# Turning the second weight by transposing transfers of pairs of 8-bit values

## The reference

```python
x = L0_attn_x                                   # (2, 16384, 1024) float32
x = x + layernorm(attention(layernorm(x), Wq, Wk, Wv, Wo))
x = x + layernorm(ffn(layernorm(x), fast_b, w_fc, w_proj, u, v, gate))

def bitlinear(x, w):                            # w: rows are output features
    scale = clip(mean(abs(w), axis=1), 1e-5)
    tern = clip(round(w / scale), -1, 1)        # -1, 0 or 1
    return x @ (tern * scale).T
def ffn(x):
    h = bitlinear(x, w_fc) + gate * (x @ v.T @ fast_b.T @ u.T)   # hidden 4096
    return bitlinear(maximum(h, 0) ** 2, w_proj)                 # back to 1024
```

## Time and profile before

| what | value |
|---|---|
| median of 3 runs | 1131.83 us (1131.32 to 1132.46) |
| the profiled execution, its own time | 1133.4 us |
| its span on the slowest core (core 0) | 1131.9 us |
| spans of the 8 cores | 1122.7 to 1131.9 us |
| mean granted TensorE clock, by core | 0.969 to 0.973 of full |
| PE busy, core 0 | 1054.5 us (93%) |
| DVE busy, ACT busy | 577.5 us (51%), 411.8 us (36%) |

### The profile page before, as it was taken

How to read it: one execution, slowest core, us unless ns; L and a number is a source line. 1 busy time by engine, 2 the same in 40 slices (tenths; PEclk the granted TensorE clock), 3 DMA queues, 4 the chain that set the end, 5 groups by cost and what they waited for, 6 DMA issues and landing times.

```text
span 1131.9 us, 16149 instructions; the slowest of 8 cores (1122.7 to 1131.9 us)
## 1 busy us (share of the span) xinstructions
PE 1054.5 (93%) x5477; PEld 494.7 (44%) x5477; DVE 577.5 (51%) x904; ACT 411.8 (36%) x761; POOL 15.9 (1%) x33
## 2 busy tenths in 40 slices
PE   3788848978999999999999999999999999999997
PEld 1222335534444444544445444454445444444443
DVE  3888789676334443454435353444435554444333
ACT  4677699324322243213422144212422243114300
POOL 0000000000000000000000000000000000000000
PEclk9988968989999999999999999999999999999999
DMA  8999997483113212231022310341005210221011
GB/s 256 209 235 226 215 232 204 117 204 113 20 38 96 91 38 38 75 106 62 1 57 67 120 38 1 93 131 60 16 19 124 101 38 1 79 70 38 1 59 54
DMA packets 61172, 105.99 MB, mean 94 GB/s; under 512 B 37261, under 2 KB 37517, under 8 KB 61092
## 3 DMA queue, kind: packets, MB, share of 16 engines
q1 hardware_dynamic: 57124, 92.63, 29.2%
q0 software_dynamic: 3728, 12.25, 6.1%
q10 hardware_dynamic: 240, 0.07, 0.0%
HBM read 87.79 MB, written 17.31 MB: 93 GB/s over the span
## 4 chain that ended last, share of the span: by engine, by line
PE 85%; DVE 5%; issue 4%; DMA 3%; ACT 1%; SPq 1%; DVEq 0%; ACTq 0%; POOLq 0%
PE fcb L449 37%; PE pjp L463 35%; PE xp L463 1%; PE xp L503 1%; PE xp L601 1%; PE xp L562 1%; PE fcb L463 1%; PE pt L433 1%; DMA r<-x 1%; DVE below L1188 1%; DMA stg<-wpj 1%; PE pjp L514 1%; DMA lrow<-ctx 1%; DMA xy<-wpj 1%; PE xp L651 0%
## 5 line engine op out<-in xcount | busy, mean ns | idle before, releaser
L449 PE MATMUL fcb<-xnT,Sfc 128*128 128x512 bf16 x2048 | 466.1, 386 | 6.0 <-DVE r L1136 3.9
L463 PE MATMUL pjp<-Spj,r 128*128 128x512 fp8e4 x1920 | 426.6, 381 | 0.0
L449 PEld LDWEIGHTS fcb<-xnT,Sfc 128*128 128x128 bf16 x2048 | 197.4, 99 | 254.5 <-issue 33.4
L463 PEld LDWEIGHTS pjp<-Spj,r 128*128 128x128 bf16 x1920 | 185.8, 98 | 222.3 <-issue 8.0
L1136 DVE TENSOR_TENSOR r<-fcb,rpp 128x512 bf16<-128x512 f32 x224 | 154.5, 691 | 242.9 <-ACT rpp L827 242.5
L827 ACT ACTIVATE rpp<-fcb,hsc 128x512 f32<-128x512 f32 x224 | 153.5, 687 | 222.3 <-PE fcb L449 220.2
L1108 DVE TENSOR_TENSOR xy<-pjp,oscb 128x512 f32<-128x512 f32 x60 | 41.3, 689 | 162.0 <-PE pjp L463 161.9
L816 ACT ACTIVATE xnT<-pt 128x1024 bf16<-128x1024 bf16 x32 | 32.7, 1020 | 138.4 <-PE pt L433 138.3
L799 ACT ACTIVATE lv<-mv,cvecs 128x1 f32<-128x1 f32 x64 | 18.8, 293 | 153.2 <-DVE mv L1081 86.0
L1113 DVE BATCH_NORM_STATS2 s<-xy 128x6 f32<-128x512 f32 x64 | 44.4, 694 | 9.4 <-DVE xy L1108 6.0
L1130 DVE TENSOR_TENSOR xy<-xy 128x1024 f32<-128x1024 f32 x32 | 39.1, 1223 | 4.3 <-DVE xy L1122 4.3
(11 more groups left out here) (143 smaller groups left out, 608.4 us busy)
## 6 DMA issues: line engine op xcount, KB each, us to landing
out<-xy SPq DMA_DIRECT2D x32, 512.0 KB, 3.0
xy<-x SPq DMA_DIRECT2D x31, 512.0 KB, 4.3
xs<-x SPq DMA_DIRECT2D x29, 512.0 KB, 4.5
xy<-wfc SPq DMA_DIRECT2D x16, 512.0 KB, 5.5
xy<-wpj SPq DMA_DIRECT2D x13, 512.0 KB, 5.7
stg<-wpj SPq DMA_DIRECT2D x11, 512.0 KB, 5.1
stg<-wfc SPq DMA_DIRECT2D x10, 512.0 KB, 5.2
xs<-wpj SPq DMA_DIRECT2D x8, 512.0 KB, 6.4
```

The costliest lines, as they stand in the source:

```text
L449: mm = te.matmul(fcb[n % 3][:, 0:TT], s_fc[:, dci * HF + hc * 128:dci * HF + hc * 128 + 128], xnT[:, dci * TT:(dci + 1) * TT], start=(dci ...
L463: mm = te.matmul(dst, r2[:, hc * TT + s * 128:hc * TT + s * 128 + 128], s_pj[:, hc * D + half * 512: hc * D + half * 512 + 512], start=(hc ...
```

## The change

The turn of the second weight leaves PE and ACT and becomes 32 more transposing transfers from SP. DVE writes `tern` of units 32 to 63 as 8-bit values, 1,024 bytes per partition; the transfer takes them for 512 columns of 16-bit values and transposes those. So two neighbouring columns of w_proj land interleaved, byte by byte, in one partition of `s_pj`; the host puts columns c and c+128 side by side beforehand, and `proj_part` reads its 512 moving columns at every second byte. `unit`, `evac` and their semaphores `p_un` and `a_ev` go. `cut(n)` now always waits for the transfer of unit n-3; PE waits for the transfers (`weights_in`) at n = 48 and ahead of `proj(0, 1)`; SP issues the last nine in a loop of its own, with the loads of `xs` between them; GpSimd's `rows(0)` waits for the last three transfers.

```diff
-        tbank = [b.bitcast(BF16) for b in pjb]
+        spj_pair = s_pj[:].bitcast(BF16).rearrange("p (c o) -> p c o", o=D)
+        spj_even = s_pj[:].rearrange("p (c o e) -> p c e o", o=D, e=2)
+        tern8 = [t[:, 0:D // 2].bitcast(FP8) for t in tern]
...
+            def turned(m):
+                if m < NFU:
+                    sync.dma_start_transpose(
+                        sfc3[:, :, m * 128:m * 128 + 128], tern[m % 3][:]
+                    ).then_inc(d_tr[m % 3], 16)
+                else:
+                    q, k = divmod(m - NFU, 4)
+                    sync.dma_start_transpose(
+                        spj_pair[:, 4 * k:4 * k + 4, q * 128:q * 128 + 128],
+                        tern[m % 3][:, 0:D // 2]
+                    ).then_inc(d_tr[m % 3], 16)
...
                 if m >= 0:
                     sync.wait_ge(v_ab, m + 1)
-                    if m < NFU:
-                        sync.dma_start_transpose(
-                            sfc3[:, :, m * 128:m * 128 + 128], tern[m % 3][:]
-                        ).then_inc(d_tr[m % 3], 16)
+                    turned(m)
...
-            sync.wait_ge(v_ab, NUNIT - 2)
-            load(xs[0], 4, d_xs[0])
-            sync.wait_ge(v_ab, NUNIT - 1)
-            load(xs[1], 5, d_xs[1])
-            sync.wait_ge(v_ab, NUNIT)
+            for m in range(NUNIT - NSLOT, NUNIT):
+                sync.wait_ge(v_ab, m + 1)
+                turned(m)
+                if m == NUNIT - 2:
+                    load(xs[0], 4, d_xs[0])
+                if m == NUNIT - 1:
+                    load(xs[1], 5, d_xs[1])
...
-            gp.wait_ge(p_un, NPU)
+            for n in range(NUNIT - 3, NUNIT):
+                gp.wait_ge(d_tr[n % 3], 16 * (n // 3 + 1))
...
-                        s_pj[:, hc * D + half * 512:
-                             hc * D + half * 512 + 512],
+                        spj_even[:, hc // 2, hc % 2,
+                                 half * 512:half * 512 + 512],
...
-            def unit(n):
-                if n > NFU + 1:
-                    te.wait_ge(a_ev, n - NFU - 1)
-                te.wait_ge(v_ab, n + 1)
-                for blk in range(DCN):
-                    cols = slice(blk * 128, blk * 128 + 128)
-                    mm = te.transpose(tbank[n % 2][:, cols],
-                                      tern[n % 3][:, cols], identb[:])
-                mm.then_inc(p_un, 1)
+            def weights_in(n):
+                for m in range(n - 3, n):
+                    te.wait_ge(d_tr[m % 3], 16 * (m // 3 + 1))
...
-                if n >= NFU:
-                    unit(n)
...
                     if m == 0:
-                        te.wait_ge(a_ev, 16)
+                        weights_in(NFU + 16)
...
-            te.wait_ge(a_ev, NPU)
+            weights_in(NUNIT)
...
-                if n >= NFU:
-                    evac(n)
...
-                if n >= NFU + 3:
-                    ve.wait_ge(p_un, n - NFU - 2)
-                elif n > 2:
+                if n > 2:
                     ve.wait_ge(d_tr[n % 3], 16 * (n // 3))
...
-                ve.scalar_tensor_tensor(tern[n % 3][:], stg[n % NSLOT][:],
+                dst, sat = ((tern[n % 3][:], None) if n < NFU else
+                            (tern8[n % 3], False))
+                ve.scalar_tensor_tensor(dst, stg[n % NSLOT][:],
...
-        "wpj": np.ascontiguousarray(np.asarray(w_proj, np.float32)),
+        "wpj": np.ascontiguousarray(np.asarray(w_proj, np.float32).reshape(
+            D, HCN // 2, 2, 128).transpose(0, 1, 3, 2).reshape(D, HF)),
```

More of the change, by code:

```diff
@@ L230, in build_nc @@
         v_lr = sem("v_lr")
-        p_un = sem("p_un")
         p_early = sem("p_early")
-        a_ev = sem("a_ev")
         p_osc = sem("p_osc")
@@ L844, in abssum @@
                               accum_out=wsum[:, n:n + 1]).then_inc(a_abs, 1)
[L846 to L852, removed]
             def out_scale(half):
@@ L1197, in cut @@
                                              ALU.is_lt))
-                ve.scalar_tensor_tensor(tern[n % 3][:], stg[n % NSLOT][:],
+                dst, sat = ((tern[n % 3][:], None) if n < NFU else
+                            (tern8[n % 3], False))
+                ve.scalar_tensor_tensor(dst, stg[n % NSLOT][:],
                                         thr[:, c:c + 1], below[n % 2][:],
-                                        ALU.is_gt,
-                                        ALU.subtract).then_inc(v_ab, 1)
+                                        ALU.is_gt, ALU.subtract,
+                                        saturate=sat).then_inc(v_ab, 1)
             def stats(g, src):
```

## The result

| what | before | after |
|---|---|---|
| median of 4 runs each | 1131.57 us | 1143.03 us (1142.17 to 1144.24) |
| ratio, 95% interval | 1 | 1.0104 (1.0092 to 1.0116) |
| profiled execution, its own time | 1133.4 us | 1143.09 us |

What follows compares the result with a forecast made beforehand. PE is held by the two large products for most of the span; DVE paces the first stage's units, PE barely behind. Start -0.5, restart +1.2, pace +4.1 give +4.8 us: median 1131.8 to 1136.6, range 1131 to 1145.

Steps and rivals of the forecast that it cites:

- What goes and what does not follow: End of first stage: 6.8 us of turning leave PE's chain, early parts end at 207.5, but proj(0, 1) awaits the last transfer.
- The pace: Cuts of the second weight: DMA share sets 2.46 us a unit against DVE's 2.28, delaying the last cut 4.1 us.
- The landing of the last transfer: Ahead of proj(0, 1): the last transfer takes 3.8 us, so the start is 0.5 us earlier, apart from the pace.
- The restart: At proj(0, 1): PE idles before it and restarts at the lower clock, costing 1.2 us.
- The zeros: Strided read, 8-bit write, later xs load, GpSimd's rows(0) and SP's issue times: each taken to cost zero.
- The strided read: Second product, line 463: reading every second byte costs zero; the rival, 4 us from 1% on, 415 if doubled, had 0.09.
- the 8-bit write: DVE's tern: 8-bit output taken to change nothing from 1284 ns; the rival of a faster write had 0.07.
- The queue saturates hard: Rival on the transfers: pace 2.73 us a unit, delay 10.4 us, +11.1 in all, 1142.9 us; chance 0.14.
- The DMA engines keep up: Rival on the transfers: pace at or below DVE's, delay 0 to 1.5 us, 1132.5 to 1134 us; chance 0.27.

Runs made afterwards that it cites:

- merged: The changed kernel with two units of the second weight sharing one buffer and one 256 KB transfer, 16 transfers in place of 32: ratio to before 1.0004.
- the hybrid: The kernel before, with PE turning units 32 to 55, transposing transfers for the last eight alone and the xs loads moved: ratio to before 1.0004.

## Why the prediction was right in sign and wrong in size

**What goes and what does not follow: right.** The turned units and evacuations left PE and ACT, the early parts ended well before the last transfer landed (212.7 against 223.2), and the 6.8 us were worth nothing. They ended 5.2 us later than the 207.5 of the text, which left the pace out there; the pause was 10.6 us all the same, not 6.

**The pace: the step that failed.** The term was 23 x (2.46 - 2.28) = 4.1 us, and the last cut came 7.0 us late on core 0, 5.7 us and more on the others. The working took the pace as a rate: shares of 2.66 us a unit over an allowed 1.08. The measured pace was indeed 2.66 us, near the upper bound of 2.73, but not as a rate: with the same bytes and one more buffer it was 2.28 to 2.42 us, with six buffers 2.28, at more GB/s and nearly the same share. The text had the deciding pair of numbers and passed over it: "about 4.8 us, are what a transfer may take", beside landings of 4.3 us at the median and 6.7 at the worst for the transfers of before. In the changed kernel a transfer landed just behind the load issued ahead of it. SP's issues of one load and the next transfer, and how long each took to land:

```profile
185.74 0.57 SPq L309 DMA_DIRECT2D stg<-wpj  x1
187.13 1.19 SPq L293 DMA_TRANSPOSE Spj<-tern  x1
```

```profile
stg<-wpj SPq DMA_DIRECT2D x1, 512.0 KB, 6.3
...
Spj<-tern SPq DMA_TRANSPOSE x1, 5.6
```

The load lands at 192.0, the transfer at 192.7; over twelve such pairs from 164 to 196 us the gap was 0.2 to 0.7 us (up to 2.1 us in a few pairs of other cores). So the time of such a transfer was here the rest of the load's, and its half size did not make it early: 5.1 us at the median where the full ones of before took 4.3. The step should have set that time against the room of three cuts. The text also counted the wrong neighbour: it took the 23 transfers with a load behind them, but the load ahead is the one that held them, and those are 24, units 32 to 55 (that of unit 55 took 6.2 us).

**The landing of the last transfer: mis-sized.** 3.8 us were taken, knowing that the `xs` load stands ahead; it was 6.0 on core 0 and 4.2 to 6.3 on the others. So the start of `proj(0, 1)`, forecast 0.5 us earlier apart from the pace, was 9.2 - 7.0 = 2.2 us later. It is the same as with the pace: DVE's first instruction that waits for that `xs` load starts at 222.10, and the transfer lands at 223.15.

**The restart: right in kind, small in size.** 1.2 us forecast, 8.77 - 7.07 = 1.7 us on core 0, 1.3 to 2.9 on the others. The sum of the three is 7.0 + 2.2 + 1.7 = 10.9 us; DVE's first instruction behind `proj(0, 1)` moved from 221.30 to 232.17, 10.9 us. The first square of the next tile moved by 9.7 us (263.80 to 273.52), as the span did by 9.6: the shift passed through to the end, less 1.2 us made up in the stage of single blocks. Of the 11.5 us between the medians the other 1.8 are how far the profiled execution of before lies above its median.

**The zeros: right.** The strided read (382 against 381 ns, 1.0002 alone) and the 8-bit write (1284 against 1284 ns). The later `xs` load brought DVE a new wait of 3.8 us for the rows of block 4, all of it inside its wait for `proj(0, 1)`. For the strided read, the Trainium skill's rule of two hits a line (SBUF — State Buffer, Specifications (TRN2)) says no cost, and this trace agrees.

**The rivals.** "The queue saturates hard" gave 1142.9, next to the measured 1143.0, by a mechanism that the buffers refute: the right time for a wrong reason. "The DMA engines keep up" was wrong for three buffers and right about the engines: with six they carried everything at DVE's pace. That is also what the rule in Advanced Engine Details and Errata of the Trainium skill, section X-Bar Transpose (TRN2), led to. On transfers with little beside them the runs come nearer to it than the shares of before did: a turned transfer of 128 KB landed in 2.4 us and a merged one of 256 KB in 3.0 at the least, so 128 KB more cost 0.6 us, where the rule gave 0.50 and the shares 0.68.

## What to carry to other kernels

A transfer that gives back a buffer must be judged by its time from cut to landing against the room that the buffers leave, not by the bytes. In these runs that time was the rest of the large load issued just ahead of it, so make the buffers one or more deeper, or keep loads that nobody needs yet behind the transfer that somebody waits for. Moving the loads to GpSimd's queue was no way out here (1.0262). A share of the DMA engines above 1 is no proof that they are full: compare the GB/s with a run that has more room.

## What the runs showed that I had not expected

- The share of the DMA engines was 1.12 at 250 GB/s (three buffers) and at 272 GB/s (six), and 1.13 at 291 GB/s (merged), each on the slowest core of its run.
- SP took 1.19 us to issue a transfer of 128 KB and 1.23 us for one of 256 KB: the issue hardly depended on the size.
- With the same loads in GpSimd's queue, a transfer took up to 14 us and the engines moved 166 to 211 GB/s, by core, in place of 242 to 260.
- PE's pauses ahead of `proj(0, 1)`, in the runs with four and six buffers, merged transfers and the hybrid: after up to 2.2 us it ran in 7.07 us with one exception in 16 (2.2 us, 8.75); after 2.5 us and more it took 8.4 to 10.0 us with four exceptions in 37 (2.6 to 3.6 us, 7.07).
